# Convolution weights of the first two images made in tap halves, high passes ahead of low ones, and an MLP order turned by half a group

## The reference

```python
# block L0: window attention (windows of 8 x 8 pixels, 8 heads of depth 8), then an MLP
xc = xc + window_attention(layernorm(xc))          # 128 windows of 64 pixels
h = layernorm(xc)
xc = xc + gelu(h @ w_mlp1 + b_mlp1) @ w_mlp2 + b_mlp2   # hidden size 256
# block L1: a gated multi-size convolution
h = einsum('bchw,oc->bohw', x, pw1_w) + pw1_b
scores = sigmoid(relu(h.mean((2, 3)) @ fc1_w.T + fc1_b) @ fc2_w.T + fc2_b)
mask = the 32 channels of each image with the largest scores
h = relu(h)
offsets = tanh(h.mean((2, 3)) @ off_w.T + off_b).reshape(B, 3, 2)
sel = (h * mask)[:, :32]                            # channels 0 to 31, masked
for i, (size, base) in enumerate([(3, dw3), (5, dw5), (7, dw7)]):
    w = base[:32] * (1 + sigmoid(offsets[:, i, 0])) + tanh(offsets[:, i, 1])   # of each image
    outs.append(depthwise_conv(sel, w, size))
out = einsum('bchw,oc->bohw', concat(outs), pw_w[:, :96]) + pw_b + x
```

## Time and profile before

| | us |
|---|---|
| three runs, median (lowest to highest) | 370.58 (366.53 to 370.76) |
| the profiled execution | 365.95 |
| its span, from first to last instruction | 364.1 |
| TensorE busy with matmuls | 325.0 (89%) |
| VectorE busy | 231.9 (64%) |
| ScalarE busy | 215.5 (59%) |
| GpSimd busy | 71.4 (20%) |

### The profile page before, as it was taken

One profiled execution on the slowest core, in us unless ns is written; L12 is line 12 of the kernel. 1 busy time (PEld: TensorE's weight loads), 2 busy tenths in 40 slices (PEclk: granted clock), 3 DMA queues, 4 the chain that ended last, 5 costly groups with the idle time before them and its releaser, 6 DMA issues.

```text
span 364.1 us, 6376 instructions
## 1 busy us (share of the span) xinstructions
PE 325.0 (89%) x2432; PEld 224.4 (62%) x2432; DVE 231.9 (64%) x376; ACT 215.5 (59%) x350; POOL 71.4 (20%) x63
## 2 busy tenths in 40 slices
PE   2567999999999999999998995999629999999994
PEld 1344676767767677676776753444127777777773
DVE  6557176386783866847758374446976799867411
ACT  6252826668476684765733587989586347646600
POOL 5371101212212122121020391123410000000000
PEclk9989999999999999999999998999959999999999
DMA  7523363322233212332132000076000657788721
GB/s 177 123 61 72 90 126 68 70 56 50 53 66 68 53 49 59 64 70 53 49 63 59 2 0 2 1 147 153 0 2 1 139 121 141 149 166 173 152 61 29
DMA packets 31147, 27.64 MB, mean 76 GB/s; under 512 B 21008, under 2 KB 27664, under 8 KB 31120
## 3 DMA queue, kind: packets, MB, share of 16 engines
q1 hardware_dynamic: 30544, 26.48, 34.6%
q10 hardware_dynamic: 576, 0.79, 0.8%
HBM read 3.78 MB, written 2.10 MB: 16 GB/s over the span
## 4 chain that ended last, share of the span: by engine, by line
PE 76%; DVE 11%; ACT 5%; DMA 3%; SPq 2%; issue 1%; POOL 1%; DVEq 0%; ACTq 0%
PE psum L1007 24%; PE psum L778 11%; PE psum L794 4%; PE psum L759 4%; PE psum L710 4%; PE psum L780 4%; PE psum L781 4%; PE psum L760 4%; PE psum L803 4%; DVE maxima L1090 3%; PE psum L923 3%; DMA probs<-in_rel_table 2%; PE psum L934 2%; PE psum L737 2%; PE psum L811 2%; PE psum L742 1%
## 5 line engine op out<-in xcount | busy, mean ns | idle before, releaser
L1007 PE MATMUL psum<-shifted,conv_w 128*128 128x512 f32 x336 | 87.4, 423 | 9.5 <-ACT conv_w L270 9.5
L1007 PEld LDWEIGHTS psum<-shifted,conv_w 128*128 128x128 f32 x336 | 65.0, 195 | 31.1 <-issue 10.3
L544 ACT ACTIVATE probs<-psum 128x512 f32<-128x512 f32 x64 | 38.3, 598 | 50.1 <-PE psum L781 49.3
L778 PE MATMUL psum<-q_heads,k_blocks 128*128 128x512 f32 x192 | 59.1, 416 | 0.0
L1090 DVE TENSOR_REDUCE maxima<-psum 128x8 f32<-128x512 f32 x64 | 41.1, 685 | 23.7 <-PE psum L760 23.7
L778 PEld LDWEIGHTS psum<-q_heads,k_blocks 128*128 128x128 f32 x192 | 34.9, 188 | 13.6 <-issue 7.1
L284 POOL TENSOR_TENSOR parts<-x,parts 128x256 fp32r<-128x256 f32 (+1 forms) x21 | 19.0, 919 | 102.1 <-ACT parts L493 57.2
L710 PE MATMUL psum<-parts,center_average 128*128 128x512 f32 x64 | 22.7, 438 | 13.7 <-DVE parts L284 12.5
L759 PE MATMUL psum<-k_heads,q_blocks 128*128 128x512 f32 x64 | 27.2, 425 | 4.7 <-DMA k_heads<-k_parts 3.3
L270 ACT CAST conv_w<-conv_w 32x896 fp32r<-32x896 f32 x32 | 30.0, 938 | 0.4
L1104 DVE RECIPROCAL inv_sum<-psum 128x256 f32<-128x256 f32 x16 | 28.0, 1749 | 3.3 <-PE psum L803 3.2
(11 more groups left out here) (138 smaller groups left out, 516.6 us busy)
## 6 DMA issues: line engine op xcount, KB each, us to landing
shifted<-images SPq DMA_DIRECT2D x32, 332.5 KB, 5.5
k_blocks<-k_parts SPq DMA_DIRECT2D x32, 128.0 KB, 2.8
q_heads<-q_parts SPq DMA_DIRECT2D x128, 32.0 KB, 1.9
k_heads<-k_parts SPq DMA_DIRECT2D x64, 32.0 KB, 1.8
out<-x SPq DMA_DIRECT2D x8, 256.0 KB, 4.8
x<-in_x SPq DMA_DIRECT2D x6, 256.0 KB, 5.9
x<-in_x SPq DMA_DIRECT2D x4, 128.0 KB, 4.7
weights<-in_weights ACTq DMA_DIRECT2D x1, 443.0 KB, 7.9
```

The costliest lines, as they stand in the source:

```text
L544: act.activation(probs[:, w, :], psum[:, PROB0 + w % 2, :], ACT.Exp).then_inc(S["ac_probs"], 1)
L778: pe.matmul(bank, k_blocks[:, w // (NW // 2), k_part, w % (NW // 2), :], q_heads[:, q_part, :, w * T:(w + 1) * T], start=k_part + q_part = ...
L1007: ins = pe.matmul(psum[:, CONV0 + bh, :], conv_w[bh][:, w_part, t, :], img[:, y:y + H - 1:2, x0:x0 + W], start=t == 0 and w_part + part == ...
```

## The change

1. TensorE's MLP order: `mlp1(2)` ahead of `centered2(NG - 1)`, `mlp2(1, 1)` ahead of `variance2(NG - 1)`, and the loop's body begins half a step later. The sequence of all other matmuls of the MLP is the same.
2. The weights of units 0 and 1 are made in two halves of 7 taps: VectorE `half_products` four times, ScalarE `high_half` four times (even cast and the odd casts from `whole_w` instead of from `conv_w`), VectorE `high_odd` (two of the odd casts of the second half) and `low_halves` (the whole low part, with all its odd casts).
3. VectorE's order: `half_products(0, 0)` ahead of `pool_image(NG - 3)` and `add_mlp(NG - 1)`; the rest of units 0 and 1, more than before, ahead of the last two pools and `gate_means(1)`.
4. In each unit the 28 passes with high weights come first, then the 14 with low ones. For units 0 and 1 each half of the high passes waits for its own weights, and the low passes for theirs. `gate_means(1)` on TensorE stands between the high and the low passes of unit 0, `gate_spread(1)` between the two halves of the high passes of unit 1.

The semaphore targets of the later units are counted two lower, since units 0 and 1 no longer use those semaphores. The diff (left out is the list of semaphore names):

```diff
@@ -656,15 +656,23 @@
                 act.activation(mem["shift"], mem["offset"], ACT.Tanh).then_inc(S["gate_act"], 1)
 
             def high_weights(u, bh):
-                act.wait_ge(S["dv_whole"], u + 1)
-                if not (isinstance(u, int) and u < 2):
-                    act.wait_ge(S["pe_conv"], u - 1)
+                act.wait_ge(S["dv_whole"], u - 1)
+                act.wait_ge(S["pe_conv"], u - 1)
                 act.copy(conv_w[bh][:, 0, :, 0:C], whole_w[:, bh]).then_inc(S["ac_high"], 1)
-                act.wait_ge(S["ac_high"], u + 1)
+                act.wait_ge(S["ac_high"], u - 1)
                 odd_row_weights(act.copy, bh, 0, range(SHIFTS))
-                act.wait_ge(S["low_weights"], u + 1)
+                act.wait_ge(S["low_weights"], u - 1)
                 odd_row_weights(act.copy, bh, 1, range(2)).then_inc(S["ac_odd"], 1)
 
+
+            def high_half(bh, half):
+
+                t = slice(half * TAP, (half + 1) * TAP)
+                act.wait_ge(S["dv_half"], 2 * bh + half + 1)
+                act.copy(conv_w[bh][:, 0, t, 0:C], whole_w[:, bh, t]).then_inc(S["ac_even_half"], 1)
+                for shift in range(1, SHIFTS - half):
+                    ins = act.copy(conv_w[bh][shift * KS:(shift + 1) * KS, 0, t, C:], whole_w[(shift - 1) * KS:shift * KS, bh, t])
+                ins.then_inc(S["ac_high_half"], 1)
 
             gelu(0, 0)
             act.wait_ge(S["pe_pv"], 2 * NG)
@@ -693,9 +701,11 @@
             relu(NG - 3, NB4 - 2, 1)
             evacuate_mlp(NG - 1, 1)
             relu(NG - 2, NB4 - 1, 0)
-            high_weights(0, 0)
+            high_half(0, 0)
             relu(NG - 1, NB4 - 1, 1)
-            high_weights(1, 1)
+            high_half(0, 1)
+            high_half(1, 0)
+            high_half(1, 1)
             gate(1)
             with act.Fori(1, NB4) as b4:
                 for bh in range(2):
@@ -966,15 +976,21 @@
             projection(NG - 1)
             mlp1(1, range(2, 4))
             mlp2(0, 0)
+            mlp1(2)
             centered2(NG - 1)
+            mlp2(1, 1)
             variance2(NG - 1)
-            with pe.Fori(0, NG // 2 - 2) as i:
-                mlp1(2 * i + 2)
-                mlp2(2 * i + 1, 1)
+            with pe.Fori(0, NG // 2 - 3) as i:
                 pointwise1(2 * i, 0)
                 mlp1(2 * i + 3)
                 mlp2(2 * i + 2, 0)
                 pointwise1(2 * i + 1, 1)
+                mlp1(2 * i + 4)
+                mlp2(2 * i + 3, 1)
+            pointwise1(NG - 6, 0)
+            mlp1(NG - 3)
+            mlp2(NG - 4, 0)
+            pointwise1(NG - 5, 1)
             mlp1(NG - 2)
             mlp2(NG - 3, 1)
             gate_means(0)
@@ -991,31 +1007,39 @@
 
 
 
-            def convolve(b4, bh, tiles=range(NKT)):
-                u = 2 * b4 + bh
-                if tiles[0] == 0:
-                    pe.wait_ge(S["po_no_row"], 2)
-                    pe.wait_ge(S["ac_odd"], u + 1)
-                    pe.wait_ge(S["dv_odd"], u + 1)
-                    pe.wait_ge(S[f"shift_in{bh}"], 16 * SHIFTS * (b4 + 1))
-                    if not (isinstance(b4, int) and b4 == 0):
-                        pe.wait_ge(S["dv_result"], u - 1)
+            def passes(bh, w_part, tiles):
+
                 for t in tiles:
                     y, x0 = t // TAP * SHIFTS, t % TAP
-                    for w_part, part in ((0, 0), (0, 1), (1, 0)):
+                    for part in range(2 - w_part):
                         img = shifted[:, bh, part, :].rearrange("p (y x) -> p y x", x=PW)
                         ins = pe.matmul(psum[:, CONV0 + bh, :], conv_w[bh][:, w_part, t, :], img[:, y:y + H - 1:2, x0:x0 + W],
                                         start=t == 0 and w_part + part == 0, stop=t == NKT - 1 and w_part == 1)
-                if tiles[-1] == NKT - 1:
-                    ins.then_inc(S["pe_conv"], 1)
-
-            convolve(0, 0, range(0, 12))
-            gate_means(1)
-            convolve(0, 0, range(12, NKT))
+                return ins
+
+            def convolve(b4, bh):
+                u = 2 * b4 + bh
+                pe.wait_ge(S["ac_odd"], u - 1)
+                pe.wait_ge(S["dv_odd"], u - 1)
+                pe.wait_ge(S[f"shift_in{bh}"], 16 * SHIFTS * (b4 + 1))
+                pe.wait_ge(S["dv_result"], u - 1)
+                passes(bh, 0, range(NKT))
+                passes(bh, 1, range(NKT)).then_inc(S["pe_conv"], 1)
+
+            def convolve_first(bh, between):
+                pe.wait_ge(S["po_no_row"], bh + 1)
+                pe.wait_ge(S[f"shift_in{bh}"], 16 * SHIFTS)
+                for half in range(2):
+                    pe.wait_ge(S["ac_high_half"], 2 * bh + half + 1)
+                    pe.wait_ge(S["dv_high_half"], bh + half)
+                    passes(bh, 0, range(half * TAP, (half + 1) * TAP))
+                    between[half]()
+                pe.wait_ge(S["dv_low_half"], bh + 1)
+                passes(bh, 1, range(NKT)).then_inc(S["pe_conv"], 1)
+
+            convolve_first(0, (lambda: None, lambda: gate_means(1)))
             gate_scores(1)
-            convolve(0, 1, range(0, 7))
-            gate_spread(1)
-            convolve(0, 1, range(7, NKT))
+            convolve_first(1, (lambda: gate_spread(1), lambda: None))
             with pe.Fori(1, NB4) as b4:
                 for bh in range(2):
                     convolve(b4, bh)
@@ -1288,21 +1312,59 @@
 
             def whole_weights(b4, bh):
                 u = 2 * b4 + bh
+                n = 2 * u + 4
                 dve.tensor_tensor(taps_window(whole_w[:, bh], 2), *factors(b4, bh, 2), ALU.mult)
                 dve.tensor_tensor(product5[:], *factors(b4, bh, 1), ALU.mult)
                 dve.tensor_tensor(product3[:], *factors(b4, bh, 0), ALU.mult).then_inc(S["dv_product"], 1)
-                dve.wait_ge(S["dv_product"], 2 * u + 1)
+                dve.wait_ge(S["dv_product"], n + 1)
                 window = taps_window(whole_w[:, bh], 1)
                 dve.tensor_tensor(window, window, product5[:], ALU.add).then_inc(S["dv_product"], 1)
-                dve.wait_ge(S["dv_product"], 2 * u + 2)
+                dve.wait_ge(S["dv_product"], n + 2)
                 window = taps_window(whole_w[:, bh], 0)
                 dve.tensor_tensor(window, window, product3[:], ALU.add).then_inc(S["dv_whole"], 1)
 
             def low_weights(b4, bh):
-                dve.wait_ge(S["ac_high"], 2 * b4 + bh + 1)
+                u = 2 * b4 + bh
+                dve.wait_ge(S["ac_high"], u - 1)
                 low_part(dve, whole_w[:, bh], conv_w[bh][:, 0, :, 0:C], conv_w[bh][:, 1, :, 0:C]).then_inc(S["low_weights"], 1)
-                dve.wait_ge(S["low_weights"], 2 * b4 + bh + 1)
+                dve.wait_ge(S["low_weights"], u - 1)
                 odd_row_weights(dve.tensor_copy, bh, 1, range(2, SHIFTS)).then_inc(S["dv_odd"], 1)
+
+            def half_products(bh, half):
+
+                def some(m):
+                    o = (TAP - KERNELS[m]) // 2
+                    shape = [128, KERNELS[m], C]
+                    tap = tap_w[:, m, bh, half * TAP + o:(half + 1) * TAP - o]
+                    return (whole_w[:, bh, half * TAP + o:(half + 1) * TAP - o],
+                            (tap.unsqueeze(2).to_broadcast(shape), fuse_w[:, m, :].unsqueeze(1).to_broadcast(shape)))
+
+                sums7, by7 = some(2)
+                sums5, by5 = some(1)
+                sums3, by3 = some(0)
+                dve.tensor_tensor(sums7, *by7, ALU.mult)
+                dve.tensor_tensor(product5[:, half], *by5, ALU.mult)
+                dve.tensor_tensor(product3[:, half], *by3, ALU.mult).then_inc(S["dv_product"], 1)
+                dve.wait_ge(S["dv_product"], 2 * (2 * bh + half) + 1)
+                dve.tensor_tensor(sums5, sums5, product5[:, half], ALU.add).then_inc(S["dv_product"], 1)
+                dve.wait_ge(S["dv_product"], 2 * (2 * bh + half) + 2)
+                dve.tensor_tensor(sums3, sums3, product3[:, half], ALU.add).then_inc(S["dv_half"], 1)
+
+            def high_odd(bh):
+
+                dve.wait_ge(S["dv_half"], 2 * bh + 2)
+                last = SHIFTS - 1
+                dve.tensor_copy(conv_w[bh][0:KS, 0, TAP:, C:], whole_w[last * KS:, bh, 0:TAP])
+                dve.tensor_copy(conv_w[bh][last * KS:, 0, TAP:, C:], whole_w[(last - 1) * KS:last * KS, bh, TAP:]).then_inc(S["dv_high_half"], 1)
+
+            def low_halves(bh):
+                for half in range(2):
+                    t = slice(half * TAP, (half + 1) * TAP)
+                    dve.wait_ge(S["ac_even_half"], 2 * bh + half + 1)
+                    ins = low_part(dve, whole_w[:, bh, t], conv_w[bh][:, 0, t, 0:C], conv_w[bh][:, 1, t, 0:C])
+                ins.then_inc(S["dv_low_even"], 1)
+                dve.wait_ge(S["dv_low_even"], bh + 1)
+                odd_row_weights(dve.tensor_copy, bh, 1, range(SHIFTS)).then_inc(S["dv_low_half"], 1)
 
             def result(b4, bh):
```

(14 more changed lines are left out.)

2 lines of the change are left out of this document (1 added, 1 removed).

## The result

The changed kernel takes 377.22 us (median of 4 runs, 375.0 to 378.49), the kernel before 369.88 (median of 4, 366.53 to 370.76). The ratio is 1.0213, 95% interval [1.0155, 1.0271]: slower by 2.1%, 7.9 us by the ratio (the medians lie 7.3 us apart). Forecast were 373.3 us, at most 377.0, and a change of +2.7 us.

The account below looks back on a forecast made before the run. It took TensorE's 9.5 us wait for ScalarE's last cast, then gate_means(1), as the bound. Gate: 279.41 - 2.25 + 2.1 + 1.65 = 280.9; span 366.8, +2.7 us; on the median 370.58 + 2.7 = 373.3 us, range 366.0 to 377.0.

Parts of the forecast that it names:

- Rival A: Convolution start: gate_means(1) holds TensorE; +2.7 us, between +1.2 and +4; chance 0.60.
- Rival D: Convolution start: gate_means(1) does not hold TensorE, early start reaches the end; 356 us, faster by over 2%; chance 0.03.
- E's mechanism: VectorE's weights: each half_products instruction costs a whole's time, 15.0 instead of 8.8 us; in sum +8.9 us; chance 0.05.
- Part 1: Turned MLP order on TensorE: moved matmuls fill its idle holes, mlp2(2, 0) and the first gate 2.25 us earlier.
- Parts 2, 3: VectorE ahead of gate_means(1): new weight work +2.1 us and collisions with GpSimd +1.65 us.
- Part 5: TensorE from the gate at 280.9: gate matmuls 0.37, low passes 3.55, lower clock 1.4, remainder 80.6 us.
- rival B: MLP: the lead is lost through the lower clock after idling before gelu(2), or a loop wait; +5 us; chance 0.16.
- Part 3: VectorE's collisions with GpSimd's low_image work while making weights: 1.65 us, between 0 and 2.3.
- Part 2: VectorE's weights of two images in halves: 17.6 us where 15.5 stood, +2.1; high_odd casts at 0.4 us each.

Follow-up runs that it names:

- E1: Kernel before with only the MLP order turned; ratio 0.9984 [0.9958, 1.0010].
- E7: Kernel before with GpSimd's memsets of images held back until the attention casts are done, and the MLP order turned; ratio 0.9894, median 365.08 us.
- E3: Kernel after with TensorE executing gate_means(1) behind the low passes of unit 0 instead of ahead of them; ratio 1.0113.
- E4: Kernel after with VectorE making the last two pools and gate_means(1) ahead of unit 1's weights; ratio 1.0125.
- E10: Kernel before with only each unit's 28 high passes put ahead of its 14 low ones; ratio 0.9983.
- E6: Kernel before with GpSimd's eight memsets of images held back until VectorE's casts at the end of attention are done; ratio 0.9896, median 365.45 us.
- E5: Kernel before, unchanged, run once more for its trace; 371.33 us.
- E2: Kernel after with the MLP order of before; ratio 1.0224 [1.0182, 1.0266].
- E11: Kernel after with memsets held back, old MLP order, only unit 0 in halves, first half behind the add, gate_means(1) later on VectorE and TensorE; 362.79 us, ratio 0.9798.
- E9: Kernel after with half_products(0, 0) back behind pool_image(NG - 3) and add_mlp(NG - 1); ratio 1.0147.
- E12: Kernel after with unit 1's weights made whole as before, unit 0's still in halves; ratio 1.0131.
- E8: Kernel after with GpSimd's memsets of images held back until the attention casts are done; ratio 1.0072.

## Why the prediction was wrong

In short: the prediction had the wait that decides, and three steps of its sum failed. It booked 2.25 us for the turned MLP order, and the turn brought nothing that shows in the medians (E1, E7); it gave the gate's data 34.4 us from gate 0, and it took 36.5, for collisions and casts; and it gave the end 85.9 us behind it, where 86.7 passed.

What was right, step by step. Rival A is what happened: TensorE starts the convolution early, does 28 passes, and stands at `gate_means(1)` longer than it stood before (10.7 us; "about 11.5" forecast), with all later units behind it. E3 and E4 show it by moving TensorE's wait and VectorE's work separately. The tail from `gate_scores(1)` on is 80.7 us where 80.6 was said; image 2's weights never became late; ScalarE was not the limit; an undisturbed `half_products` takes 2.2 us (265.46 to 267.70). The order of the passes costs nothing (E10). Rival D did not occur. E's mechanism did not either, since a half costs 2.2 us and not 3.75; but its outcome, slower by over 2%, is where the median lies (2.1%, between 1.6% and 2.7%), and it was given 0.05.

The sum failed because four terms were mis-sized, all on the same side. In the traces the forecast end was 366.8, the measured 373.2, 6.4 us more:

| Step | forecast | measured | difference |
|---|---|---|---|
| Part 1: gate 0 on TensorE, time in the span | 246.5 | 250.0 | +3.5 |
| Parts 2, 3: gate 0 to `gate_means(1)` ready | 34.4 | 36.5 | +2.1 |
| Part 5: gate 1 ready to the end | 85.9 | 86.7 | +0.8 |

*Part 1, the step that failed outright.* "I do not book the full 4.3 us" was right, and the 2.25 us booked were still too many. The reasoning moved matmuls into TensorE's holes and kept the holes' ends where they were. But a hole's end is the moment when the waiting instruction's data comes, and the moved matmuls stand ahead of that instruction: in E7 `centered2` is late by 1.1 us through `mlp1(2)` alone, and in the kernel after `variance2` is late because `mlp2(1, 1)` ran at the lower clock, 3.02 us instead of 1.94. Then `mlp1(3)` idles 2.67 us for `gelu(2)`, whose start hangs on `variance2`. The prediction had `gelu(2)` 0.5 us earlier by the turn, since `variance2` would run at the upper clock; that it did (0.74 us), but it started 1.0 us later. So `gelu(2)` came later with the turn: 14.5 us after the start of `mlp1(0)` in E7 and 13.5 in E6, 19.4 in the kernel after and 18.9 in E5. In the kernel after `mlp2(2, 0)` started at 233.3 and not near 229.8. From `mlp1(0)` to gate 0:

| | casts 5.9 us | casts 0.85 us |
|---|---|---|
| MLP order of before | 41.1 (E5), 41.1 (E10), 40.7 (E2) | 34.1 (E6), 34.2 (E11) |
| turned | 40.8 (E1), 39.3 (after), 39.4 (E3), 39.2 (E4), 39.4 (E9), 39.2 (E12) | 35.7 (E7), 35.8 (E8) |

So in the traces the turn gives 0 to 1.9 us where the casts make the holes long, and takes 1.6 where they are short; in the medians no difference is clear of noise either time. This is rival B, which the prediction gave 0.16: it named the clock and an idle stretch ahead of `gelu(2)`, and its sign, `mlp2(2, 0)` near 232, came (233.3, some 2.8 of it by the casts, below). Its clock is shown for a part of the traces only: behind the 2.67 us, `mlp1(3)` took 3.42 us in E7 and 2.87 in E1, but 2.38 in the kernel after, at the upper level. What held in every trace is the late `gelu(2)`.

*The baseline.* 2.8 of the 3.5 us are no effect of the change. The two casts of VectorE at the end of attention took 5.88 us, not the 3.08 of the trace of before:

```profile
213.05 5.88 DVE L1152 CAST normed<-rstd 64x512 fp32r<-64x512 f32 x2
218.96 1.40 DVE L284 TENSOR_TENSOR normed<-rstd,normed 64x512 fp32r<-64x512 f32 x2
```

GpSimd's memsets run from 208.04 to 218.06, and the casts end only when these have: the first waits for all the rest of them. E5 shows the same in the kernel before, and E6 and E8 that it costs both kernels about 4 to 5 us. The prediction saw that the median lay 4.6 us above the profiled execution and laid the change on the median, which took care of the level; but it did not ask which row of the trace was the lucky one, though a cast that takes 1.5 us in one group and 0.4 in all others was in that trace. With the baseline's 2.8 us off and the 0.9 us by which attention ended earlier in the trace after, 1.6 us of part 1 remain as the change's own. That takes the 2.8 us one for one, which is not shown: in the order of before, 5.9 us of casts came with 3.9 us more from `mlp1(0)` to gate 0 (37.2, and 41.1 in E5), because behind the longer idle `centered2` took 1.22 us instead of 0.74 and `mlp1(2)` 3.62 instead of 2.98. By E5 0.4 us remain; by the medians, in which the turn gave nothing, the whole 2.25.

*Part 3, collisions: 1.65 us forecast, 3.05 measured.* Three places carry one microsecond too much: 1.62 instead of 0.62 (against GpSimd's 259.39), 1.38 instead of 0.36 (against 262.33) and the pair of L284 2.18 instead of 1.16 (against 269.06). The first was priced and the third at half, and `low_image(NG - 2)` was not thought of: undisturbed, the first half would have ended at 261.75, before GpSimd's 262.33, but the first collision had delayed it. The rule of the Trainium skill that the prediction weighed ("SBUF — State Buffer", Who interferes with whom) gave 2.3; it was nearer than my 1.65, and the trace agrees with it in each of the three cases. It agrees too in that the memset of `no_row`, from 260.59 to 261.42, did not lengthen the product at 261.05 (0.48 us, as undisturbed). The upper bound of 2.3 was no bound, as a delay can make the next collision.

*Part 2, casts: 0.4 us taken, 0.61 measured* for `high_odd` (L1357, L1358), while a cast of the same 32 x 448 in `low_halves` (L272) takes 0.42. Four casts of 0.2 us are the 0.8 missing. The ends for this term were 0.31 and 0.62, and it lay at the upper one. The Trainium skill has a rule that would give this ("VectorE: DVE Perf Modes", What auto-detection actually checks): with a single source, and source and destination in SBUF, the mode of two elements a cycle that these casts can have is taken if the outermost dimensions of both, other than of size one, are both even or equal. The source in `whole_w` is 448 contiguous values, its target 7 rows of 64; L272's source and target are both 7 rows. If the contiguous rows count as one dimension, the rows agree with the rule; neither that nor that it is the cause was tried.

*Part 5, the tail.* After 11 us of idle the lower clock also held for the gate's own matmuls: 0.88 us for 0.37, and the 14 passes took 5.10 us where 4.95 was said. How long it holds differs between executions: the same 14 passes took 5.5 us in E8, 5.9 in E12 and 6.0 in E2, so that this term alone is uncertain by 0.9 us.

Sum for the change itself, with part 1 by the medians: 2.7 + 2.25 (part 1) + 2.1 (parts 2 and 3) + 0.8 (part 5) = 7.85 us, against 7.9 measured (5.7 to 10.0 by the interval); with 1.6 for part 1 it is 7.2. That it meets the measured to the tenth is chance, given the interval. VectorE's work for the two units, without collisions, is 18.4 us (21.4 less 3.05) where 17.6 were forecast and 15.5, waits and collisions included, stood before.

## What to carry to other kernels

Before an early start is booked, list what stands in the engine's queue behind it that waits for something else; here one small gate, whose data came no earlier, took back the whole start, and splitting the work in front of that data made it worse. A hole in an engine's timeline is not free room: work moved ahead of the waiting instruction delays it whenever it is longer than the hole, and the clock behind an idle stretch makes it longer than the rows say. And compare the same instruction with its siblings in the trace: the one cast at 1.5 us among casts at 0.4 was the sign of a collision worth 1% to both kernels.
